# Two-layer mixture kernel: skip sums from two parts, block products summed in pairs, experts' tail rows and rotated keys in other ways, and three changed orders

## The chip, the cores and the metric

The kernel runs on one core of one Trainium2 chip. The metric is the device time of one execution in microseconds (us). All data is fp32.

## The reference

Input x is 16 batches of 256 positions and 512 channels. Four layers follow each other, each on a layer norm of the sum so far.

```python
# 1. gated long convolution: for each of 32 groups of 8 rows
kv = v[:, :, :, None, :] * x2[:, :, None, :, :]            # 8 x 8 products
y  = irfft(rfft(kv) * rfft(k))[..., :L] + kv * skip        # causal convolution, and a skip term
out = einsum('bhijl,bhil->bhjl', y, x1)                    # weighed sum over i
# 2. mixture of 8 experts (the best 2 by gates) and a shared expert
# 3. attention with compressed keys and a rotated part, 16 heads, 9 positions of look-back
k_rope = rope(kv_c @ W_kr)
# 4. dense feed-forward: 512 -> 2048 -> 512, gelu
```

## The kernel before

Each engine has one written-out stream of instructions, with waits on counters. Matmuls that must be exact to fp32 are either one fp32 matmul or three fp32r matmuls: an operand is split into a high part (a copy rounded to fp32r) and a low part (the difference), and high x high, low x high and high x low are summed.

**Convolution.** `NHC` = 32 steps h. A step has two halves u and four output blocks lb of 128 positions, so eight blocks y; each block has its own bank of four `m.Y`. ScalarE norms the rows (`norm`), TensorE turns them (`turn_v`), GpSimd forms the products kf (`product`, L1246), ScalarE their high part kh (`split`), and VectorE or GpSimd the low part kl (`low`, L961 and L1251). TensorE convolves (`conv`, L508 to L516). VectorE's `gather_i` multiplies a block by the context (L971) and reduces over i (L977); TensorE's `turn_out` and VectorE's `finish` make the rows. The skip term is apart: VectorE's `weigh` makes w = xn * skip * ctx (L949), TensorE multiplies w by a fixed 0/1 matrix in fp32 (`skip_sums`, L495), and `skips` multiplies by the context. GpSimd adds the input (`residual`, L1233). Statistics of step h+2 are VectorE's (`stats`, L928 to L932), their power GpSimd's (`power`, L1217). The finished rows of earlier steps are normed (`stats_rows`, `shift_rows`, `norm_rows`), turned (`turn_rows`, L534), and give gate logits, from which `best` and, every eight steps, `choose` pick two experts and their gates.

In a step, VectorE's order is written by hand:

```python
if u == 1 and lb == 2 and h + 2 < NHC: stats(h + 2)
if u == 0 and lb == 0 and more: weigh(h + 1)
if u == 1 and lb == 3 and h + 2 < NHC: shift(h + 2)
gather_i(h, u, lb, UNITS[n] if n < len(UNITS) and lb == 0 else None)   # L971, low, L977
```

**Experts.** After the shared expert (`hidden`, `second`, with `ranks`, `by_head` and `biases` set between its 64 blocks), 71 tiles of 128 rows go through their expert (`tile_first`, `turn_hidden`, `tile_second`, L710). The tile's second bias is gathered into one of four buffers (`tile_bias`, L1346), which the store of four tiles ago must have left, and `tile_out` adds to it (L1194).

**Attention.** 16 batches of 16 heads; TensorE's stream runs scores, turns and sums of successive heads, with the projections of later heads or batches between. Three banks pass from user to user in the order of `misc_order`. In batch 0 the weights of each head are made as well, from factors that SyncE loads into a ring (`factors`, L1461; `weights`, L1682 to L1685). SyncE also stores the mixed rows (`keep`, L1466). `krope` (L1576) makes the keys' rotated part.

**Dense.** 8 groups of 16 blocks; the next group's rows are normed and turned (`dense_stats`, `dense_norm`, `dense_turn`, L2316) beside blocks 3 to 11 of the present one.

Of the kernel before, what the change touches and what calls it, by code (L numbers as in the profile page):

```python
# [96 lines left out]
def front_memory(nc, ctx, m):  # L97
# [48 lines left out]
    m.z = c("z", [128, 3, 512])  # L146
# [31 lines left out]
    c("pad", [128, 3688])  # L178
# [12 lines left out]
    keep("gap", [128, 544])  # L191
    w1 = keep("w1", [128, 2, NE, 1024], F32R)
# [14 lines left out]
def attention_memory(nc, ctx, m):  # L207
# [4 lines left out]
    t("gap", [128, 512])  # L212
# [52 lines left out]
    m.pr = t("pr", [128, 2, 2, 256])  # L265
    m.smf = m.sm[:, :, :].rearrange("p a b -> p (a b)")
# [76 lines left out]
def sync_front(sp, w, K):  # L343
# [93 lines left out]
    for n in range(STEPS + 2):  # L437
# [40 lines left out]
def tensor_front(pe, w, K):  # L478
# [75 lines left out]
    skip_sums(0)  # L554
    for h in range(NHC):
        more = h < LAST
        for u in range(2):
            for lb in range(4):
# [83 lines left out]
    for n in range(STEPS + 2):  # L642
# [14 lines left out]
        if n == 9:  # L657
            by_head()
        if n == 11:
# [73 lines left out]
def scalar_front(ac, w, K):  # L733
# [17 lines left out]

    def turned_v(h):
# [52 lines left out]
    for n in range(4):  # L805
        split(*UNITS[n])
    for h in range(NHC):
        more = h < LAST
        for u in range(2):
            for lb in range(4):  # L810
# [15 lines left out]
                if u == 1 and lb == 0 and h > 8 and h % 8 == 1:  # L826
                    choose(h // 8 - 1)
                if h == LAST and u == 1 and lb in (1, 2):
                    shared_rows(lb - 1)
                if h and u == 1 and lb == 2:  # L830
                    norm_rows(h - 1)
                if h == LAST and u == 1 and lb == 3:
# [23 lines left out]
    for n in range(STEPS + 2):  # L856
# [10 lines left out]
        if n == 9:  # L867
# [3 lines left out]
        if n == 11:  # L871
# [47 lines left out]
def vector_front(ve, w, K):  # L919
# [23 lines left out]
    def weigh(h):  # L943
# [4 lines left out]
        w.wait_ge(*PE["psk", h - 2])  # L948
# [14 lines left out]
    def gather_i(h, u, lb, between):  # L963
# [44 lines left out]
    def choose(c):  # L1008
# [13 lines left out]
        ve.tensor_tensor(cv, m.oh[:, 0, r, :], m.oh[:, 1, r, :], ALU.add).then_inc(*VE("cnt", c))  # L1022
        w.wait_ge(*AC["exp", c])
# [17 lines left out]
    filter_lo()  # L1041
    w.wait_ge(*GP["onef"])
# [7 lines left out]
    skips(0)  # L1050
    for h in range(NHC):
        more = h < LAST
        for u in range(2):
            for lb in range(4):
# [14 lines left out]
                if u == 1 and lb == 0 and h > 8 and h % 8 == 1:  # L1069
                    choose(h // 8 - 1)  # L1070
                if h == LAST and u == 1 and lb == 0:
# [74 lines left out]
    for n in range(STEPS + 2):  # L1146
# [63 lines left out]
def gpsimd_front(gp, w, K):  # L1210
# [71 lines left out]
    for n in range(4):  # L1282
# [3 lines left out]
        if n == 2:  # L1286
            residual(0)
# [53 lines left out]
    def tile_bias(j):  # L1341
        w.wait_ge(*Q[f"y{j % 4}"]["ys", j - 4])
# [28 lines left out]
def misc_order():  # L1371

    out = [("keys", 0), ("values", 0), ("krope", 0)]
# [4 lines left out]
    for h in range(4):  # L1378
        weights(h)
    out.extend([("turn", 0, 0), ("turn", 0, 1)])  # L1380
# [73 lines left out]
def sync_attention(sp, w, K):  # L1454
# [54 lines left out]
    keep(1)  # L1509
    for N in range(TOTAL + 4):  # L1510
# [22 lines left out]
def tensor_attention(pe, w, K):  # L1533
# [154 lines left out]
    values(0)  # L1688
    krope(0)
    for h in range(4):  # L1690
# [56 lines left out]
def scalar_attention(ac, w, K):  # L1747
# [78 lines left out]
    w.wait_ge(*K.PE["m2", TILES - 1])  # L1826
    keys(0)
# [54 lines left out]
def vector_attention(ve, w, K):  # L1882
# [159 lines left out]
    w.wait_ge(*K.PE["m2", TILES - 1])  # L2042
    keys(0)
# [91 lines left out]

def gpsimd_attention(gp, w, K):
# [51 lines left out]
    rope_weights()  # L2188
# [160 lines left out]
def sync_dense(sp, w, K):  # L2349
# [285 lines left out]
```

## Time and profile before

| | |
|---|---|
| timed runs | 3155.25, 3163.14, 3162.99 us, median 3162.99 |
| profiled execution | 3159.11 us, span 3157.4 us |
| TensorE busy | 3094.9 us (98%) |
| VectorE busy | 2206.7 us (70%) |
| ScalarE busy | 1216.9 us (39%) |
| GpSimd busy | 1157.0 us (37%) |
| granted TensorE clock, mean | 0.995 of full speed |
| DMA | 87 GB/s over the span |

The shares are averages over four unlike stages. Between 56 and 580 us, in the convolution, TensorE is busy 519.3 us of 524, VectorE 480.5, GpSimd 461.9 and ScalarE 170.4. A row's "idle before" names what ended the engine's wait. Successive instructions of an engine overlap a little, so the place that one takes is the distance from its start to the next one's start.

### The profile page before, as it was taken

What the parts mean: (1) busy time and instruction counts of PE and PEld (TensorE: products, weight loads), DVE (VectorE), ACT (ScalarE), POOL (GpSimd) and SP (SyncE); (2) the same over time, 40 slices, a digit from 0 to 9 for tenths busy, and PEclk for the clock granted to TensorE, in tenths of its full rate; (3) what the DMA queues carried; (4) which work ended last, traced back from release to release, by engine and by line L of the source; (5) the groups of instructions that cost most, each with busy time, mean ns of one, the idle gap of its engine ahead of it and who ended that gap; (6) DMA issues with size and microseconds to landing.
All of it is one profiled execution on the core that took longest, in us unless ns stands there. A gap on an engine that the chain in (4) does not pass through costs nothing.

```text
span 3157.4 us, 49339 instructions
## 1 busy us (share of the span) xinstructions
PE 3094.9 (98%) x18197; PEld 2652.9 (84%) x18197; DVE 2206.7 (70%) x5732; ACT 1216.9 (39%) x2882; POOL 1157.0 (37%) x1176
## 2 busy tenths in 40 slices
PE   8999999999999789999999999999999999999999
PEld 5667676789899579999999999999998788888887
DVE  7999999756555678888888888888888433333332
ACT  3333333333444345555555555555555311111111
POOL 8988888455344422222222222222201011100110
PEclk9999999999999999999999999999999999999999
DMA  4444432288677621111111111111101200000000
GB/s 144 141 126 142 124 118 87 74 281 306 213 229 227 228 74 55 48 48 41 47 48 48 48 48 42 40 48 42 40 28 57 87 27 27 27 27 27 28 14 14
DMA packets 124973, 277.67 MB, mean 88 GB/s; under 512 B 18312, under 2 KB 18960, under 8 KB 124736
## 3 DMA queue, kind: packets, MB, share of 16 engines
q1 hardware_dynamic: 95712, 178.54, 17.7%
q0 software_dynamic: 29024, 95.97, 9.1%
q8 instruction: 148, 2.42, 0.3%
q14 instruction: 89, 0.73, 0.1%
HBM read 170.04 MB, written 104.42 MB: 87 GB/s over the span
## 4 chain that ended last, share of the span: by engine, by line
PE 91%; DVE 4%; DMA 2%; POOL 1%; ACT 1%; issue 1%; SPq 0%; POOLq 0%; DVEq 0%
PE f_Y L508 5%; PE t_U L1673 4%; PE t_U L1674 4%; PE g_O L2404 4%; PE g_O L2403 4%; PE g_O L2402 4%; PE g_PH L2388 4%; PE g_PH L2390 4%; PE t_U L1675 4%; PE g_PH L2389 4%; PE t_T L1649 3%; PE f_Y L514 3%; PE f_Y L516 3%; PE f_Y L513 3%; PE t_PO L1659 2%; PE t_PO L1660 2%
## 5 line engine op out<-in xcount | busy, mean ns | idle before, releaser
L1798 ACT ACTIVATE t_pr<-t_sm,t_nb 128x256 f32<-128x256 f32 x512 | 256.6, 502 | 407.8 <-DVE t_nb L2003 407.8
L2169 POOL TENSOR_TENSOR t_r<-t_r 128x256 f32<-128x256 f32 x128 | 94.7, 740 | 741.4 <-DVE t_r L1982 419.9
L2460 DVE CAST g_hh<-g_hf 128x512 fp32r<-128x512 f32 x128 | 62.2, 486 | 408.2 <-PE g_O L2404 404.4
L1246 POOL TENSOR_TENSOR c_kf<-c_vt,c_ct 128x512 f32<-128x512 f32 x256 | 297.5, 1179 | 4.4 <-PE f_Y L508 4.4
L2431 ACT ACTIVATE g_hf<-g_PH,b1g 128x512 f32<-128x512 f32 x128 | 88.2, 689 | 501.1 <-PE g_PH L2390 501.1
L2013 DVE TENSOR_SCALAR t_pr<-t_pr,t_rw 128x256 f32<-128x256 f32 x512 | 239.8, 468 | 18.1
L513 PE MATMUL f_Y<-c_kh,c_th 128*128 128x512 f32 x448 | 224.1, 500 | 4.8 <-ACT c_kh L737 2.8
L2388 PE MATMUL g_PH<-g_xh,g_w 128*128 128x512 f32 x512 | 202.6, 396 | 0.0
L1673 PE MATMUL t_U<-t_voh,t_oth 128*128 128x512 f32 x512 | 202.3, 395 | 0.0
L1674 PE MATMUL t_U<-t_voh,t_otl 128*128 128x512 f32 x512 | 201.6, 394 | 0.0
L1675 PE MATMUL t_U<-t_vol,t_oth 128*128 128x512 f32 x512 | 200.5, 392 | 0.0
L2390 PE MATMUL g_PH<-g_xl,g_w 128*128 128x512 f32 x512 | 199.9, 390 | 0.0
L2389 PE MATMUL g_PH<-g_xh,g_w 128*128 128x512 f32 x512 | 199.7, 390 | 0.0
L2404 PE MATMUL g_O<-g_w,g_hh 128*128 128x512 f32 x512 | 199.3, 389 | 0.0
L2402 PE MATMUL g_O<-g_w,g_hh 128*128 128x512 f32 x512 | 199.2, 389 | 0.0
L2403 PE MATMUL g_O<-g_w,g_hl 128*128 128x512 f32 x512 | 199.2, 389 | 0.0
L2003 DVE CUSTOM_DVE_ANT_0 t_sm<-t_S,t_mk 128x256 f32<-128x256 f32 x512 | 194.3, 416 | 4.5 <-PE t_S L1641 3.2
L508 PE MATMUL f_Y<-c_kf,c_t 128*128 128x512 f32 x384 | 185.4, 591 | 0.0
L1751 ACT ACTIVATE t_pth<-t_T 128x512 fp32r<-128x512 f32 x256 | 152.8, 597 | 74.2 <-PE t_T L1649 72.7
L977 DVE TENSOR_REDUCE c_R<-c_z 128x64 f32<-128x512 f32 x256 | 174.9, 683 | 6.7
L2017 DVE TENSOR_TENSOR t_ptl<-t_T,t_pth 128x512 fp32r<-128x512 f32 x256 | 175.3, 685 | 3.9 <-ACT t_pth L1751 1.4
L516 PE MATMUL f_Y<-c_kl,c_th 128*128 128x512 f32 x448 | 178.0, 397 | 0.0
(340 smaller groups left out, 9765.5 us busy)
## 6 DMA issues: line engine op xcount, KB each, us to landing
xs<-c_zero SPq DMA_DIRECT2D x71, 256.0 KB, 4.5
f_xg<-xs SPq DMA_DIRECT2D x71, 256.0 KB, 3.4
ys<-f_yt POOLq DMA_DIRECT2D x71, 256.0 KB, 3.4
f_xg<-xn SPq DMA_DIRECT2D x40, 256.0 KB, 5.3
c_xt<-x SPq DMA_DIRECT2D x32, 256.0 KB, 3.5
c_cr<-ctx SPq DMA_DIRECT2D x32, 256.0 KB, 3.9
c_ct<-ctxh SPq DMA_DIRECT2D x32, 256.0 KB, 4.5
c_t<-kt SPq DMA_DIRECT2D x32, 256.0 KB, 4.8
```

What stands on the lines that cost most here:

```text
L508: t = pe.matmul(Y, m.t[:, h % 3, c], m.kf[:, v, mb, :], start=False, stop=mb == lb)
L513: pe.matmul(Y, m.th[:, s, c], m.kh[:, v, mb, :], start=mb == 0, stop=False)
L1246: gp.tensor_tensor(o, iv, ic, ALU.mult).then_inc(*GP("kv", n))
L1673: pe.matmul(o, m.oth[:, N % 3, tt], m.voh[:, h, :], start=h == 0, stop=False)
L1674: pe.matmul(o, m.otl[:, N % 3, tt], m.voh[:, h, :], start=False, stop=False)
L1675: i = pe.matmul(o, m.oth[:, N % 3, tt], m.vol[:, h, :], start=False, stop=h == NH - 1)
L2388: pe.matmul(o, m.w1[0][k][:, kk, :], m.xh[:, s, kk, :], start=kk == 0, stop=False)
L2389: pe.matmul(o, m.w1[1][k][:, kk, :], m.xh[:, s, kk, :], start=False, stop=False)
L2390: i = pe.matmul(o, m.w1[0][k][:, kk, :], m.xl[:, s, kk, :], start=False, stop=kk == 3)
L2402: pe.matmul(o, m.hh[:, n % 2, c], m.w2[0][k], start=k == 0, stop=False)
L2403: pe.matmul(o, m.hl[:, n % 2, c], m.w2[0][k], start=False, stop=False)
L2404: i = pe.matmul(o, m.hh[:, n % 2, c], m.w2[1][k], start=False, stop=k == BLOCKS - 1)
```

## The change

- `skip_sums`: w is split into wh (ScalarE, `weighed_hi`) and wl (VectorE, `weighed_lo`), and two fp32r matmuls with the 0/1 matrix replace the fp32 one.
- `gather_i`: the product buffers are four, and one reduction sums two blocks' products after every second block.
- `choose` moves two or three blocks later, and its second half is a function of its own, `gates`, one step later still (block 1 of step 10, 18, 26). In the shared stage `by_head`, `biases` and what goes with them move from blocks 9 and 11 to 11 and 13.
- The last four tiles' bias rows are gathered into buffers of their own, after the last tile's first product.
- `krope`: six fp32r matmuls from split weights (`wkh`, `wkl`) and the split keys that exist already, for two in fp32; in batch 0 it follows the weights of head 0.
- Orders: the low part of the rotation weights is made in the tiles' stage (`rope_weights_lo`); batch 0's mix, statistics and norm are interleaved; `keep(1)` follows four factor loads; a group's dense turns are three blocks later; the dense b2 and second rows are loaded behind one more weight fetch.

```diff
 # tensor_front
     def skip_sums(h):
-        w.wait_ge(*GP["ones"])
-        w.wait_ge(*VE["w", h])
+        w.wait_ge(*VE["ones"])
+        w.wait_ge(*AC["wsh", h])
         w.wait_ge(*VE["sx", h - 1])
-        pe.matmul(m.PSK[:, :], m.ones_b, m.w[:, h % 2, :], start=True, stop=True).then_inc(*PE("psk", h))
+        pe.matmul(m.PSK[:, :], m.ones_r, m.wh[:, h % 2, :], start=True, stop=False)
+        w.wait_ge(*VE["wsl", h])
+        pe.matmul(m.PSK[:, :], m.ones_r, m.wl[:, h % 2, :], start=False, stop=True).then_inc(*PE("psk", h))
...
-        if n == 9:
+        if n == 11:
             by_head()
-        if n == 11:
+        if n == 13:
             biases()
 # scalar_front
+    def weighed_hi(h):
+        s = h % 2
+        w.wait_ge(*VE["w", h])
+        w.wait_ge(*PE["psk", h - 2])
+        copy(m.wh[:, s, :], m.w[:, s, :]).then_inc(*AC("wsh", h))
...
+                if u == 0 and lb == 0 and more:
+                    weighed_hi(h + 1)
 # vector_front
+    def weighed_lo(h):
+        s = h % 2
+        w.wait_ge(*AC["wsh", h])
+        ve.tensor_tensor(m.wl[:, s, :], m.w[:, s, :], f32(m.wh[:, s, :]), ALU.subtract).then_inc(*VE("wsl", h))
...
-        zz = m.z[:, y % 3, :].rearrange("p (b j i) -> p b j i", i=8, j=8)
+        zz = m.z[:, y % 4, :].rearrange("p (b j i) -> p b j i", i=8, j=8)
         w.wait_ge(*PE["y", y])
-        w.wait_ge(*VE["red", y - 3])
+        w.wait_ge(*VE["red", (y - 4) | 1])
         ve.tensor_tensor(zz, iv, ic, ALU.mult).then_inc(*VE("z", y))
         if between:
             low(*between)
+        if lb % 2 == 0:
+            return
...
-        rr = m.R[:, s, lb, 64 * u:64 * u + 64].rearrange("p (b j) -> p b j", j=8)
-        ve.tensor_reduce(rr, zz, AXX, ALU.add).then_inc(*VE("red", y))
+        z2 = m.z[:, y % 4 - 1:y % 4 + 1, :].rearrange("p q (c i) -> p q c i", i=8)
+        ve.tensor_reduce(m.R[:, s, lb - 1:lb + 1, 64 * u:64 * u + 64], z2, AXX, ALU.add).then_inc(*VE("red", y))
...
+                if u == 0 and lb == 2 and more:
+                    weighed_lo(h + 1)
...
-                if u == 1 and lb == 0 and h > 8 and h % 8 == 1:
+                if u == 1 and lb == 3 and h > 8 and h % 8 == 1:
                     choose(h // 8 - 1)
+                if u == 0 and lb == 1 and h > 8 and h % 8 == 2:
+                    gates(h // 8 - 1)
 # gpsimd_front
     for n in range(4):
         product(*UNITS[n])
         if n == 1:
             low(*UNITS[n])
-        if n == 2:
-            residual(0)
...
     def tile_bias(j):
-        w.wait_ge(*Q[f"y{j % 4}"]["ys", j - 4])
+        if j < TILES - 4:
+            w.wait_ge(*Q[f"y{j % 4}"]["ys", j - 4])
+        else:
+            w.wait_ge(*PE["m1", TILES - 1])
...
     for n in range(TILES + LAG):
-        if LAG - 2 <= n < TILES + LAG - 2:
+        if LAG - 2 <= n < TILES - 1:
             tile_bias(n - LAG + 2)
+        if n == TILES - 1:
+            for j in range(TILES - 4, TILES):
+                tile_bias(j)
         if n >= LAG:
             tile_store(n - LAG)
+        if n == TILES:
+            rope_weights_lo(gp, w, K)
 # sync_attention
     load(1)
-    keep(1)
     for N in range(TOTAL + 4):
...
         if N + EARLY + 2 < NH:
             factors(N + EARLY + 2)
+        if N == 3:
+            keep(1)
 # tensor_attention
     def krope(b):
-        w.wait_ge(*A["kc", b])
+        w.wait_ge(*A["wkh"])
+        w.wait_ge(*V["wkl"])
+        w.wait_ge(*A["kh", b])
+        w.wait_ge(*V["kl", b])
         M = take("krope", b)
         for z in range(2):
-            i = pe.matmul(M[:, 256 * z:256 * z + 256], m.wkr[:, z, :], m.kc[:, :], start=True, stop=True)
+            o = M[:, 256 * z:256 * z + 256]
+            pe.matmul(o, m.wkh[:, z, :], m.kch[:, s, :], start=True, stop=False)
+            pe.matmul(o, m.wkl[:, z, :], m.kch[:, s, :], start=False, stop=False)
+            i = pe.matmul(o, m.wkh[:, z, :], m.kcl[:, s, :], start=False, stop=True)
 # vector_attention
     mix(0, 0)
+    stats(0, 0)
     mix(0, 1)
-    stats(0, 0)
+    norm(0, 0)
     stats(0, 1)
-    norm(0, 0)
     norm(0, 1)
 # tensor_dense
-            if g + 1 < GROUPS and k in (5, 7, 9, 11):
-                dense_turn(pe, w, K, 4 * (g + 1) + (k - 5) // 2)
+            if g + 1 < GROUPS and k in (8, 10, 12, 14):
+                dense_turn(pe, w, K, 4 * (g + 1) + (k - 8) // 2)
```

## Rows read from the trace of the kernel before

**Rows 1.** Waits of TensorE, whole span: us in total, times, longest.

```profile
PE t_M L1554 <- DVE t_r L1914: 9.0, 1, 9.0
PE t_M L1682 <- DMA t_xo<-fac: 8.2, 1, 8.2
...
PE f_PV L534 <- ACT c_xb L789: 6.1, 4, 1.6
PE f_Y L710 <- DVE f_yt L1194: 5.4, 4, 1.7
PE f_PV L623 <- DVE f_idc L1122: 2.9, 1, 2.9
...
PE g_PM L2316 <- DVE g_xn L2295: 2.4, 1, 2.4
```

**Rows 2.** The chain in order of time, convolution: start us, us, what.

```profile
65.62 0.23 PE f_Y L513
...
409.73 0.86 PE f_PSK L495 x2
...
463.62 0.86 PE f_PSK L495 x2
```

**Rows 3.** Timeline of VectorE, one step: start us, us, instruction, idle before.

```profile
403.02 0.88 DVE L961 TENSOR_TENSOR c_kl<-c_kf,c_kh 128x512 fp32r<-128x512 f32 x1 [1.02 <-ACT c_kh L737]
403.82 0.68 DVE L977 TENSOR_REDUCE c_R<-c_z 128x64 f32<-128x512 f32 x1
404.42 0.68 DVE L971 TENSOR_TENSOR c_z<-f_Y,c_ct 128x512 f32<-128x512 f32 x1
405.13 0.69 DVE L977 TENSOR_REDUCE c_R<-c_z 128x64 f32<-128x512 f32 x1
...
407.22 0.69 DVE L971 TENSOR_TENSOR c_z<-f_Y,c_ct 128x512 f32<-128x512 f32 x1
...
410.08 1.15 DVE L961 TENSOR_TENSOR c_kl<-c_kf,c_kh 128x512 fp32r<-128x512 f32 x1
411.16 0.67 DVE L977 TENSOR_REDUCE c_R<-c_z 128x64 f32<-128x512 f32 x1
...
415.73 0.15 DVE L932 TENSOR_SCALAR c_rs<-c_ag 128x1 f32<-128x1 f32 x1
...
420.98 0.88 DVE L961 TENSOR_TENSOR c_kl<-c_kf,c_kh 128x512 fp32r<-128x512 f32 x1 [1.03 <-ACT c_kh L737]
```

**Rows 4.** Timeline of GpSimd, the same step.

```profile
406.03 1.06 POOL L1246 TENSOR_TENSOR c_kf<-c_vt,c_ct 128x512 f32<-128x512 f32 x1
407.36 2.10 POOL L1246 TENSOR_TENSOR c_kf<-c_vt,c_ct 128x512 f32<-128x512 f32 x2 [0.26 <-PE f_Y L508]
409.41 1.28 POOL L1227 TENSOR_TENSOR c_tl<-c_t,c_th 128x512 fp32r<-128x512 f32 x1
410.65 1.73 POOL L1251 TENSOR_TENSOR c_kl<-c_kf,c_kh 128x512 fp32r<-128x512 f32 x1
...
415.96 0.55 POOL L1217 TENSOR_TENSOR c_rs<-c_rs,mhalf 128x1 f32<-128x1 f32 x1 [1.45 <-DVE c_rs L932]
```

**Rows 5.** Timeline of VectorE, an operation of 256 elements.

```profile
1062.65 0.41 DVE L1941 TENSOR_TENSOR t_kvl<-t_M,t_kvh 128x256 fp32r<-128x256 f32 x1
```

**Rows 6.** Timelines of VectorE and GpSimd: low parts beside GpSimd.

```profile
28.19 4.24 DVE L961 TENSOR_TENSOR c_kl<-c_kf,c_kh 128x512 fp32r<-128x512 f32 x1
...
118.99 1.28 POOL L1227 TENSOR_TENSOR c_tl<-c_t,c_th 128x512 fp32r<-128x512 f32 x1
...
119.02 1.79 DVE L961 TENSOR_TENSOR c_kl<-c_kf,c_kh 128x512 fp32r<-128x512 f32 x1
```

**Rows 7.** Timeline of VectorE, end of a choose.

```profile
193.82 1.27 DVE L1028 TENSOR_TENSOR f_gac<-c_sm,f_gac 128x8 f32<-128x8 f32 x1
```

**Rows 8.** Timeline of GpSimd, the attention's first gather.

```profile
1065.76 1.00 POOL L2149 DMA_INDIRECT t_xT<-ys,idx  x1 [2.52 <-DMA ys<-f_yt]
```

**Rows 9.** Waits of SyncE, 1030 to 1130 us.

```profile
SPq L81 <- POOL t_xt L2160: 24.2, 1, 24.2
```

More of the change, by code:

```diff
@@ L177, in front_memory @@
     m.ob = c("ob", [8, 2, 512])
-    c("pad", [128, 3688])
+    m.wh = c("wh", [128, 2, 512], F32R)
+    m.wl = c("wl", [128, 2, 512], F32R)
+    m.ones_r = c("ones_r", [128, 128], F32R)[:, :]
+    c("pad", [128, 1000])
     sw = c("sw", [128, 8192], F32R)
@@ L191, in front_memory @@
     keep("gap", [128, 544])
+    with ExitStack() as late:
+        sb(nc, late, "f_gap3", [128, 13168])
+        m.yx = sb(nc, late, "f_yx", [128, 4, 512])
     w1 = keep("w1", [128, 2, NE, 1024], F32R)
@@ L210, in t @@
         return sb(nc, ctx, f"t_{name}", shape, dt)
-    t("gap", [128, 512])
+    t("gap", [128, 256])
+    m.wkl = t("wkl", [128, 2, 128], F32R)
     with ExitStack() as low:
@@ L337, in turn_at, with out_rows, bias_landed @@
     return None
+def out_rows(m, j):
+    return m.yt[:, j % 4, :] if j < TILES - 4 else m.yx[:, j % 4, :]
+def bias_landed(j):
+    return f"v{j % 4}" if j < TILES - 4 else f"vx{j % 4}"
 def sync_front(sp, w, K):
@@ L553, in tensor_front @@
     turn_v(0)
-    skip_sums(0)
     for h in range(NHC):
@@ L565, in tensor_front @@
                     skip_sums(h + 1)
+                if u == 0 and lb == 2 and h == 0:
+                    skip_sums(0)
                 if u == 0 and lb == 0 and h > 1:
@@ L804, in scalar_front @@
     turned_v(0)
-    for n in range(4):
-        split(*UNITS[n])
+    split(*UNITS[0])
+    split(*UNITS[1])
+    weighed_hi(0)
     for h in range(NHC):
@@ L831, in scalar_front @@
                     norm_rows(h - 1)
+                if u == 1 and lb == 3 and h > 8 and h % 8 == 1:
+                    choose(h // 8 - 1)
                 if h == LAST and u == 1 and lb == 3:
@@ L1022, in choose, with gates @@
         ve.tensor_tensor(cv, m.oh[:, 0, r, :], m.oh[:, 1, r, :], ALU.add).then_inc(*VE("cnt", c))
+    def gates(c):
+        r = slice(8 * c, 8 * c + 8)
+        S_ = m.sm[:, c % 2, :, :]
         w.wait_ge(*AC["exp", c])
@@ L1049, in vector_front @@
     low(0, 0, 0)
-    skips(0)
+    weighed_lo(0)
     for h in range(NHC):
@@ L1064, in vector_front @@
                     finish(h - 1)
+                if u == 0 and lb == 2 and more:
+                    weighed_lo(h + 1)
+                if u == 0 and lb == 3 and h == 0:
+                    skips(0)
                 if u == 1 and lb == 1 and more:
@@ L1068, in vector_front @@
                     best(h - 2)
-                if u == 1 and lb == 0 and h > 8 and h % 8 == 1:
+                if u == 1 and lb == 3 and h > 8 and h % 8 == 1:
                     choose(h // 8 - 1)
+                if u == 0 and lb == 1 and h > 8 and h % 8 == 2:
+                    gates(h // 8 - 1)
                 if h == LAST and u == 1 and lb == 0:
@@ L1159, in vector_front @@
             choose(3)
+        if n == 6:
+            gates(3)
         if n == 8:
@@ L1308, in gpsimd_front @@
                     filter_lo(h + 1)
+                if u == 1 and lb == 0 and h == 0:
+                    residual(0)
                 if u == 1 and lb == 2 and more:
@@ L1371, in misc_order @@
 def misc_order():
-    out = [("keys", 0), ("values", 0), ("krope", 0)]
+    out = [("keys", 0), ("values", 0)]
     def weights(h):
@@ L1379, in misc_order @@
         weights(h)
+        if h == 0:
+            out.append(("krope", 0))
     out.extend([("turn", 0, 0), ("turn", 0, 1)])
@@ L1688, in tensor_attention @@
     values(0)
+    weights(0)
     krope(0)
-    for h in range(4):
+    for h in range(1, 4):
         weights(h)
@@ L2130, in vector_attention, with rope_weights_lo @@
             dense_turned_lo(ve, w, K, 3)
+def rope_weights_lo(gp, w, K):
+    m = K.t
+    w.wait_ge(*K.A["wrah"])
+    gp.tensor_tensor(m.wrl[:, :], m.wqr[:, 0, :], f32(m.wra[:, :]), ALU.subtract).then_inc(*K.G("wra"))
 def gpsimd_attention(gp, w, K):
@@ L2368, in sync_dense @@
             dense_fetch(sp, w, K, k + 6)
+        if n == 0:
+            w.wait_ge(*P["vo", TOTAL - 1, 1])
+            w.wait_ge(*V["add", 2 * B - 1])
+            w.wait_ge(*Q["to"]["out", B - 1])
+            sp.dma_start(m.b2s[:, :], K.d["f1b2"]).then_inc(*Q["gb1"]("b2"))
+            load(1)
         if n >= 2 and (n - 2) % BLOCKS == BLOCKS - 1 and (n - 2) // BLOCKS + 2 < GROUPS:
@@ L2426, in scalar_dense @@
             dense_weights_hi(ac, w, K, k + 3)
-        if g + 1 < GROUPS and k in (5, 7, 9, 11):
-            dense_turned_hi(ac, w, K, 4 * (g + 1) + (k - 5) // 2)
+        if g + 1 < GROUPS and k in (8, 10, 12, 14):
+            dense_turned_hi(ac, w, K, 4 * (g + 1) + (k - 8) // 2)
         w.wait_ge(*P["dph", n])
@@ L2468, in gpsimd_dense @@
         g, k = divmod(n, BLOCKS)
-        if n < DSTEPS and g + 1 < GROUPS and k in (3, 5, 7, 9):
-            dense_power(gp, w, K, 4 * (g + 1) + (k - 3) // 2)
+        if n < DSTEPS and g + 1 < GROUPS and k in (6, 8, 10, 12):
+            dense_power(gp, w, K, 4 * (g + 1) + (k - 6) // 2)
         if n < 2:
@@ L2535 @@
               "cc", "n0", "n1", "w0", "w1", "ti", *(f"g{i}" for i in range(RING)), "q0", "q1", "a0", "a1", *(f"s{i}" for i in range(RING)),
-              *(f"l{i}" for i in range(4)), *(f"y{i}" for i in range(4)), *(f"v{i}" for i in range(4)),
+              *(f"l{i}" for i in range(4)), *(f"y{i}" for i in range(4)), *(f"v{i}" for i in range(4)), *(f"vx{i}" for i in range(4)),
               "tx", "tct", "tsg", "to", "txo", *(f"tyg{i}" for i in range(4)), "tx2", "tc", "tc2", "tw0", "tw1", *(f"tm{i}" for i in range(4)),
```

50 lines of the change are left out of this document (24 added, 26 removed).

## Prediction

> **What bounds the kernel now.** The page came first: TensorE is busy almost all the span (the table above), so a change pays only if it takes time from TensorE's own stream or from its waits. The table of waits for TensorE puts 34 us of its idle time on six lines [rows 1]; the rest is small. Then I read the convolution (to about 590 us) as a chain in order of time. One channel step h takes (463.62 - 409.73)/3 = 17.96 us. TensorE is hardly ever idle in it but for three waits of 1.6 at L534. The skip product, one fp32 matmul of 512 columns, holds it 0.86, an fp32r one 0.23 [rows 2].
>
> Who comes second in that stage decides this change. VectorE's timeline over one step [rows 3] and GpSimd's [rows 4] show a closed loop. VectorE ends the variance for step h+2 at 415.73 + 0.15 = 415.88. GpSimd sat 1.45 us waiting for it, then makes in order the power, a product, a residual sum and the product that ScalarE splits; 5.10 after the variance VectorE starts that product's low part c_kl (420.98), having waited 1.02. Call K the start of this c_kl (403.02), T the start of the fourth block's product (407.22). K to T is 4.20; the places of its instructions make 4.02 (c_kl 0.80, three reductions of 0.60, two products of 0.71), so 0.18 is waiting for TensorE. T to the variance's end is 8.66; then 5.10. The loop alone turns in 17.78, only 0.18 quicker than TensorE. The change has to be judged by both.
>
> **Convolution, TensorE.** Fp32 skip product to two fp32r: 0.86 - 2 x 0.234 = 0.39 less per step, 17.57 if nothing else binds.
>
> **Convolution, VectorE.** A reduction of 512 takes a place of 0.60 (403.82 to 404.42), a product and the wait of the reduction behind it 0.71 (404.42 to 405.13) [rows 3]. 256 elements more cost 0.27 (0.68 against 0.41, [rows 5]), so a paired reduction takes 0.60 + 2 x 0.27 = 1.14; its bounds are 0.87 (nothing for the fixed part twice over) and 1.20 (two of now). `weighed_lo` has the form of c_kl: two operands in SBUF, 0.80 at the least disturbed.
>
> But such a subtraction waits for GpSimd. C_kl at 410.08 took 1.15: GpSimd was in a subtraction until 410.65, and VectorE's next instruction came 0.51 after that [rows 3, 4]. At 119.02 it came 0.03 after GpSimd's subtraction had begun and took 1.79; at 28.19 it took 4.24 [rows 6]. The Trainium skill, "SBUF — State Buffer", section "Who interferes with whom", says that a VectorE instruction with two SBUF inputs and a GpSimd one that reads SBUF exclude each other, the second waiting in full. By that rule, the trace agrees: 1.15 and 1.79; without it the sum below would be 17.4 and TensorE's 17.57 the bound, with it 19.33.
>
> The new order from K, with GpSimd's product at K + 3.01 to 4.07 (406.03) [rows 4]:
> - c_kl 0.80, product and paired reduction 0.71 + 1.14, product 0.60: `weighed_lo` is reached at K + 3.25, inside GpSimd's product. It gets its turn at 4.07; T comes 0.51 later, K + 4.58.
> - From T to the next c_kl were 2.86; the reduction in between grows by 0.54: 3.40, so K + 7.98. GpSimd goes on 0.41 to 0.45 after VectorE took its turn (its subtraction at 410.65 took 1.73 instead of 1.28): two products 2.05 and a subtraction 1.24 end at 7.77 to 7.82, and the next subtraction holds until 9.06. C_kl misses the gap by 0.15 to 0.2, waits until 9.06, and what follows starts at 9.57.
> - From there to the variance's end were 415.88 - 411.16 = 4.72; a reduction goes (-0.60), another grows (+0.54): 4.66, so 14.23. Then 5.10 as before: weigh comes at 2.6 after the variance, as now, and `weighed_hi` on ScalarE is over before the split. K' = K + 19.33.
>
> VectorE's loop would set the period at 19.33, 1.37 longer than now. TensorE would wait 19.33 - 17.57 = 1.76 per step, at L534, the one line of the loop at which it already waits. In steps 1 to 8 GpSimd has one more subtraction in that place; the same sum gives 19.3. The loop exists where step h+2 has statistics: 29 turns, +39.7. The last two steps gain 0.39 each, TensorE ends about 1.2 ahead of VectorE, the head gains perhaps 1 by the moved residual sum (bounds +4 and -4, the wait of 4.24 is there): -3.0.
>
> **Choose and gates.** Choose's chain on VectorE delays the rows' shift and makes three of the four waits at L534, 4.7 of 6.1 [rows 1]. They go. But three times 1.6 (gates; its last product alone is 1.27 [rows 7]) now stand in the loop, and some 0.7 (an estimate: five small instructions) where choose pushes weigh back: 6.9 - 4.7 = +2.2.
>
> Convolution: 39.7 - 3.0 + 2.2 = +38.9.
>
> **`by_head`, `biases`.** TensorE waits 2.9 for the places [rows 1]; two blocks later they are long there: -2.9. What is late next is nothing in the trace before the tiles.
>
> **Experts' tail, first turn.** The last four tiles' bias rows no longer wait for a store four tiles back; they are four gathers in a row on GpSimd, about 1.3 each, behind the last first product. Of the 5.4 at L710 the first two waits stay, the last two (2.3) go. The stores queue behind these gathers and the moved 2.35 us subtraction of rotation weights, and still end about 4 earlier, so the attention's first gather (1065.76, waiting for the last landing [rows 8]) does too. VectorE is free some 3 earlier, mixes without that subtraction beside it, and norms after one statistic instead of two. The wait of 9.0 at L1554 shrinks and starts earlier: -5.6 for both, bounds -2.3 (only L710) and -11.3.
>
> **Store of the mixed rows.** The 8.2 at L1682 is for a factor load stuck on SyncE behind `keep(1)`, which waits 24.2 for GpSimd's mix [rows 1, 9]. Four factor loads pass it now. Late next is VectorE, a step or so of 1 us behind, and the stored rows before batch 1's first norm: -7.5, bounds -4 and -9.
>
> **Rotated keys.** Two fp32 products of 256 columns (as many as one of 512, 0.86) become six fp32r of 256 (half of 0.234): 0.70. 16 batches: -2.6 (bounds 0 and -3.5). The new waits, c_kch and its low part, are two heads old by then.
>
> **Dense.** The 2.4 at L2316 goes, the turns being three blocks later; five half-steps remain before their use: -2.4. The fetch set ahead of b2 lies under a busy TensorE: 0.
>
> Outside the convolution: -2.9 - 5.6 - 7.5 - 2.6 - 2.4 = -21.0. With +38.9: +17.9. The profiled execution took 3159.1 (span 3157.4 and 1.7 around it), inside the three timed runs, whose median is 3163.0: 3159.1 + 17.9 = 3177.0.
>
> **Rivals.**
> - The next c_kl catches the gap. 0.15 to 0.2 us decide, near the error of my places; a paired reduction under 0.95 would do. Loop 4.58 + 3.40 + 0.51 + 4.66 + 5.10 = 18.25, +0.29 x 29 = 8.4; total 3159.1 + 8.4 - 0.8 - 21.0 = 3145.7. For it: most c_kl show 0.88. Against: the sum.
> - VectorE does not wait in these two places; TensorE's 17.57 binds. 29 x -0.39, choose's 4.7 and 1 of the head: -17; 3121, faster. It decides if lock waits are below 0.15 per step in sum.
> - The waits are of the 4.24 kind: one more operation of GpSimd (1.24) in a third of the steps, +12: 3189.
> - The gains after the convolution are half, because a transfer or VectorE follows up: 3187.
>
> Chances: forecast 0.53, gap caught 0.18, no waits 0.14, long waits 0.08, half gains 0.07. The forecast's own range is 3168 to 3186. Over all, without the second rival and the far end of the third: 3138 to 3192. Within 0.3% (9.5 us) is what a measurement of this kernel can't tell from no change. Faster: 0.14 and 0.11 of the 0.18, 0.25; same: the rest of it and a little of the forecast's low end, 0.10; slower 0.65.
>
> **What would show it.** Skip products at 0.23 each; 19.3 from one step's skip product to the next against 17.96; a wait at L534's turn in nearly every step, for ScalarE's c_xb; `weighed_lo` at 1.4, the c_kl of the first unit at 1.6 to 1.8; no waits at the places of L623, L1682 (8.2) and L2316; L1554 at 4 to 6. I am wrong if c_kl and the new subtraction show 0.88: then the period is below 18.2.

## The result, and the profile after

The changed kernel takes 3192.7 us (median of four runs, 3190.5 to 3195.3); the kernel before, beside it, 3162.6. The ratio is 1.0103, with a 95% interval of 1.0090 to 1.0116: slower by 30 us, where +17.9 was forecast. Its profiled execution took 3195.3 (span 3192.5), 36.2 more than that of before: the one is the longest of its four, the other lies 3.4 under its median, so 6 of these 36 are the choice of executions.

The waits of TensorE in the changed kernel, whole span (us in total, times, longest):

```profile
PE f_PV L553 <- ACT c_xb L815: 44.6, 30, 1.8
PE t_M L1615 <- DVE t_r L1985: 7.3, 2, 6.2
PE f_PT L505 <- ACT c_xn L770: 7.3, 1, 7.3
PE f_PSK L512 <- DVE c_sk L990: 5.6, 1, 5.6
```

L553 is L534 of before [rows 1]: four waits (6.1 in all) have become thirty (44.6). The waits of L623, of L1682 (8.2) and of L2316 are gone, and L1554, now L1615, still stands for 7.3. L505's 7.3 is nothing new: it is at the program's start, and before had 7.5 there (L488), which [rows 1] leave out. L512's 5.6 is new.

One step on VectorE, changed kernel, from one K to the next:

```profile
433.86 0.88 DVE L995 TENSOR_TENSOR c_kl<-c_kf,c_kh 128x512 fp32r<-128x512 f32 x1 [1.02 <-ACT c_kh L757]
...
435.37 1.22 DVE L1013 TENSOR_REDUCE c_R<-c_z 128x128 f32<-128x1024 f32 x1
...
437.10 1.37 DVE L984 TENSOR_TENSOR c_wl<-c_w,c_wh 128x512 fp32r<-128x512 f32 x1
438.39 0.68 DVE L1005 TENSOR_TENSOR c_z<-f_Y,c_ct 128x512 f32<-128x512 f32 x1
...
441.78 1.68 DVE L995 TENSOR_TENSOR c_kl<-c_kf,c_kh 128x512 fp32r<-128x512 f32 x1
443.38 0.68 DVE L1024 BATCH_NORM_STATS2 c_st<-c_xt 128x6 f32<-128x512 f32 x1
...
447.89 0.15 DVE L961 TENSOR_SCALAR c_rs<-c_ag 128x1 f32<-128x1 f32 x1
...
453.13 0.88 DVE L995 TENSOR_TENSOR c_kl<-c_kf,c_kh 128x512 fp32r<-128x512 f32 x1 [1.02 <-ACT c_kh L757]
```

And GpSimd in the same step:

```profile
440.38 1.29 POOL L1277 TENSOR_TENSOR c_tl<-c_t,c_th 128x512 fp32r<-128x512 f32 x1
441.63 1.28 POOL L1301 TENSOR_TENSOR c_kl<-c_kf,c_kh 128x512 fp32r<-128x512 f32 x1
```

Set beside [rows 3, 4]: `weighed_lo` (L984) is reached at K + 3.24 (forecast 3.25), T at K + 4.53 (4.58), the next c_kl at K + 7.92 (7.98). The gap between GpSimd's two subtractions was at 441.63; c_kl came 0.15 later and took 1.68, until the second one was over. The variance ends at K + 14.18 (14.23), K returns after 19.27 (19.33). The skip products, 0.23 each as forecast:

```profile
439.74 0.39 PE L512 MATMUL f_PSK<-c_wh,c_ones_r 128*128 128x512 f32 x1
439.97 0.39 PE L514 MATMUL f_PSK<-c_wl,c_ones_r 128*128 128x512 f32 x1
459.04 0.39 PE L512 MATMUL f_PSK<-c_wh,c_ones_r 128*128 128x512 f32 x1
```

The places are 0.23 apart, the duration 0.39 overlaps the next. The table says in which stage time was lost or won: how much later than in before the same instruction of TensorE starts, from the timelines of the profiled executions (us; the experiments' columns are read below).

```
                                  after    e1    e4    e5    e6    e7   e10
end of convolution (last L553)    +45.3  +5.5  -0.8  -1.0  +0.3  +0.2  -0.4
last shared product               +41.1  +0.8  -5.5  -4.6  -4.1  -4.3  -5.1
tiles: last first product         +41.6  +3.3  -5.3  -1.5  -2.4  -1.5  -2.0
first latent keys                 +40.1  +1.7  -4.0  -1.1  -3.2  -1.7  -1.5
turn(0,0)                         +40.4  +2.0  -3.7  -0.7  -5.6  -1.4  -2.0
first scores                      +42.8  +2.9  -2.6  +0.2  -3.6  -0.4  -0.8
keys of batch 2                   +41.6  -3.0  -6.1   0.0  -7.6  -5.6  -6.7
last scores                       +39.3  -5.2  -8.4  -2.2  -9.8  -7.8  -9.0
end                               +35.1  -9.4 -12.6  -6.4 -14.0 -12.0 -13.2
```

### The profile page after: what moved, and what is told of

Its sections match the earlier page's. It is cut to its first block, busy times and chain, and to the rows that moved or that the text cites. A ratio compares the mean times of both kernels' runs of the same rounds, so it can differ in the third digit from the quotient of the medians.

```text
span 3192.5 us, 49352 instructions
## 1 busy us (share of the span) xinstructions
PE 3088.6 (97%) x18229; PEld 2652.3 (83%) x18229; DVE 2249.0 (70%) x5638; ACT 1235.2 (39%) x2915; POOL 1157.6 (36%) x1176
## 4 chain that ended last, share of the span: by engine, by line
PE 75%; DVE 17%; POOL 4%; DMA 2%; ACT 1%; issue 1%; SPq 0%; POOLq 0%; DVEq 0%
DVE c_R L1013 4%; PE g_PH L2463 4%; PE g_PH L2465 4%; PE g_PH L2464 4%; PE g_O L2479 4%; PE g_O L2478 4%; PE g_O L2477 4%; PE t_U L1741 4%; PE t_U L1742 4%; PE t_U L1743 4%; PE t_T L1717 3%; DVE c_z L1005 3%; POOL c_kf L1296 2%; DVE c_kl L995 2%; PE t_S L1706 2%; PE t_PO L1727 2%
## 5 line engine op out<-in xcount | busy, mean ns | idle before, releaser
L2535 DVE CAST g_hh<-g_hf 128x512 fp32r<-128x512 f32 x128 | 54.7, 427 | 430.3 <-PE g_O L2479 426.6
L1296 POOL TENSOR_TENSOR c_kf<-c_vt,c_ct 128x512 f32<-128x512 f32 x256 | 306.2, 1217 | 0.0
L2084 DVE TENSOR_SCALAR t_pr<-t_pr,t_rw 128x256 f32<-128x256 f32 x512 | 241.9, 473 | 18.1
L532 PE MATMUL f_Y<-c_kh,c_th 128*128 128x512 f32 x448 | 212.0, 473 | 4.5 <-ACT c_kh L757 4.5
L533 PE MATMUL f_Y<-c_kh,c_tl 128*128 128x512 f32 x448 | 178.4, 398 | 0.0
```

The lines of the kernel that those rows point to most:

```text
L1296: gp.tensor_tensor(o, iv, ic, ALU.mult).then_inc(*GP("kv", n))
L2084: ve.tensor_scalar(m.pr[:, N % 2, t, :], m.pr[:, N % 2, t, :], m.rw[:, k4, 1:2], None, ALU.mult).then_inc(*V("nm", x))
```

## The experiments

There are fourteen, labelled e1 to e15 (there is no e8); the tenth kernel of some expectations is e10. Each ratio is against the kernel before run beside it; that one's medians lay between 3158.9 and 3159.9.

**e1, the skip product in fp32 again.** `weighed_hi` and `weighed_lo` go with it; the paired reductions stay.

```diff
     def skip_sums(h):
-        w.wait_ge(*AC["wsh", h])
+        w.wait_ge(*VE["w", h])
-        pe.matmul(m.PSK[:, :], m.ones_r, m.wh[:, h % 2, :], start=True, stop=False)
-        pe.matmul(m.PSK[:, :], m.ones_r, m.wl[:, h % 2, :], start=False, stop=True)
+        pe.matmul(m.PSK[:, :], m.ones_b, m.w[:, h % 2, :], start=True, stop=True)
```

> The changed kernel with the skip product as before (one fp32 product of 0.86 on TensorE, no weighed_hi, no weighed_lo), all else as changed, paired reductions too. The theory (weighed_lo waits for a GpSimd product and pushes the next c_kl past its gap): without it the fourth block's product comes at K + 3.25 and VectorE's loop needs 0.80 + 2.45 + 3.40 + 0.9 + 4.66 + 5.10 = 17.3, so TensorE's 17.96 binds again: period 17.9 to 18.0, some 37 us less than the changed kernel, 3152 to 3160. Rival (the paired reductions alone lengthen VectorE's part, since the one that holds c_kl back is now 1.2 long): period stays above 18.8, 3178 or more.

Measured: 3148.5, ratio 0.9966 (0.9953 to 0.9978), 44 less than the changed kernel and 3.5 under the range. Skip products come 17.97 apart from step 10 on, as the theory said, but for the steps with a choose; in steps 4 to 9 every second one is 18.4 to 18.5. The fp32r product, meant to save 0.39 a step, costs 1.31 through its low part.

**e2, one reduction for each block, the skip product split.**

```diff
-        if lb % 2 == 0:
-            return
-        z2 = m.z[:, y % 4 - 1:y % 4 + 1, :].rearrange("p q (c i) -> p q c i", i=8)
-        ve.tensor_reduce(m.R[:, s, lb - 1:lb + 1, 64 * u:64 * u + 64], z2, AXX, ALU.add)
+        rr = m.R[:, s, lb, 64 * u:64 * u + 64].rearrange("p (b j) -> p b j", j=8)
+        ve.tensor_reduce(rr, zz, AXX, ALU.add)
```

> The changed kernel with one reduction for each block instead of the pairs; the skip product stays split. The theory (a gap between two GpSimd subtractions is missed by 0.2 us): T comes at K + 4.58 as in the changed kernel, but c_kl of the next step is reached at T + 2.86 = K + 7.44, takes the gap at 7.8, and the period is 18.1 to 18.3, 28 us less than the changed kernel, 3160 to 3168. Rival (no gap, VectorE is simply short of time): the four single reductions cost as much as the two paired ones, period 19.2 to 19.4, 3190 to 3197.

Measured: 3178.0, ratio 1.0055 (1.0039 to 1.0072), between the two ranges. Steps 2 to 9 take 18.11 (one 17.67), as the sum has it; from step 10 on 18.2 and 19.35 come mixed. VectorE of e2, two of those later steps, and the GpSimd product that starts in each as `weighed_lo` is reached:

```profile
248.13 0.88 DVE L995 TENSOR_TENSOR c_kl<-c_kf,c_kh 128x512 fp32r<-128x512 f32 x1 [1.02 <-ACT c_kh L757]
252.16 0.68 DVE L984 TENSOR_TENSOR c_wl<-c_w,c_wh 128x512 fp32r<-128x512 f32 x1
255.62 0.99 DVE L995 TENSOR_TENSOR c_kl<-c_kf,c_kh 128x512 fp32r<-128x512 f32 x1
...
266.35 0.88 DVE L995 TENSOR_TENSOR c_kl<-c_kf,c_kh 128x512 fp32r<-128x512 f32 x1 [1.02 <-ACT c_kh L757]
270.37 1.62 DVE L984 TENSOR_TENSOR c_wl<-c_w,c_wh 128x512 fp32r<-128x512 f32 x1
274.76 1.20 DVE L995 TENSOR_TENSOR c_kl<-c_kf,c_kh 128x512 fp32r<-128x512 f32 x1
...
285.69 0.88 DVE L995 TENSOR_TENSOR c_kl<-c_kf,c_kh 128x512 fp32r<-128x512 f32 x1 [1.02 <-ACT c_kh L757]
```

```profile
252.16 1.61 POOL L1294 TENSOR_TENSOR c_kf<-c_vt,c_ct 128x512 f32<-128x512 f32 x1
...
270.37 1.07 POOL L1294 TENSOR_TENSOR c_kf<-c_vt,c_ct 128x512 f32<-128x512 f32 x1
```

`weighed_lo` is reached at K + 4.03 and 4.02, both times within 0.01 of the start of a GpSimd product. Once it slips in and takes 0.68, and it is the product that gets longer (1.61; K to K 18.22); once it waits and takes 1.62 (K to K 19.34). What the trace can't tell apart decides over 1.1: neither theory's one period, but a knife's edge, and the mechanism is who gets the turn, not VectorE's load, which is the same in both steps.

**e3 and e9, the low part in the shadow.** `weighed_lo(h + 1)` is moved from behind the third block to just ahead of the c_kl at K, where VectorE waits 1.02 for ScalarE; e9 has single reductions and choose in its old place as well.

```diff
+        if u == 0 and lb == 0 and h < LAST:
+            weighed_lo(h + 1)
         if between:
             low(*between)
```

> The changed kernel with weighed_lo moved from behind the third block to where VectorE waits 1.02 us for ScalarE, just ahead of the c_kl at K. The theory (the loop runs over VectorE from K to the variance; what stands between the variance and K is in the shadow of GpSimd and ScalarE): K comes at most 0.5 later, T at K + 3.25, period 17.6 to 17.9, 3140 to 3155. Rival (any two-operand subtraction of VectorE costs its wait wherever it stands, and GpSimd is held up by it): period 18.8 or more, over 3178.

> The changed kernel with weighed_lo in the shadow, one reduction per block, and choose where it was (no gates). Theory: VectorE's loop before, where TensorE did not hold it, turned in 17.65; the low part in the shadow adds nothing to 0.1, so the period is TensorE's 17.57 to 17.75, 0.2 to 0.4 less than before in 29 steps, and the time 3136 to 3144. Rival (K comes late enough that c_kl meets GpSimd's product, as in the pairs' version): 18.0 to 18.1, 3150 or so.

Measured: e3 3157.9, ratio 0.9991 (0.9982 to 1.0001), period 18.04; e9 3157.5, ratio 0.9987 (0.9977 to 0.9996), period 18.11. So the place of one instruction is worth 35 us here, with the same load on VectorE, but both are above the 17.9 and 17.75 that I expected, and e3 3 over its range in time: K comes in its old place after the variance (5.08), but the low part ahead of it had held up GpSimd's three products (4.46 in all, 4.03 in the changed kernel), so c_kl meets one and takes 1.33. For e9 the rival's period was right, its time 7 too low.

**e12, a low part with one operand.** `weighed_lo` is a plain copy of c_w; the kernel leaves the subtraction out, so its skip sums are not those of the reference.

```diff
-        ve.tensor_tensor(m.wl[:, s, :], m.w[:, s, :], f32(m.wh[:, s, :]), ALU.subtract)
+        ve.tensor_copy(m.wl[:, s, :], m.w[:, s, :])
```

> The changed kernel with weighed_lo replaced by a plain copy of c_w into the same tile (one operand in SBUF instead of two; the low part is then not what the reference needs). Theory (only an instruction with two SBUF operands waits for GpSimd's): the copy takes 0.6 at most and never waits, T at K + 3.7 to 3.9, c_kl of the next step reached at K + 7.2, in or just ahead of the gap at 7.3 to 7.8, period 17.6 to 18.2. Rival (VectorE's share of the step is too large, lock or no lock): 18.8 to 19.3.

Measured: 3182.8 (one run), period 19.0. VectorE and GpSimd of e12:

```profile
426.95 0.88 DVE L995 TENSOR_TENSOR c_kl<-c_kf,c_kh 128x512 fp32r<-128x512 f32 x1 [1.02 <-ACT c_kh L757]
...
430.20 1.11 DVE L984 CAST c_wl<-c_w 128x512 fp32r<-128x512 f32 x1
...
434.61 1.68 DVE L995 TENSOR_TENSOR c_kl<-c_kf,c_kh 128x512 fp32r<-128x512 f32 x1
```

```profile
433.22 1.29 POOL L1277 TENSOR_TENSOR c_tl<-c_t,c_th 128x512 fp32r<-128x512 f32 x1
434.47 1.27 POOL L1301 TENSOR_TENSOR c_kl<-c_kf,c_kh 128x512 fp32r<-128x512 f32 x1
```

My theory fell in its first half: a copy with one SBUF operand waits too (1.11; where nothing was in its way it took 0.42). The second half held: c_kl missed the gap at 434.47 by 0.14 and paid 1.68. The period is the rival's (18.8 to 19.3), but not for its reason: without the copy's wait of 0.7, c_kl would by this sum have come 0.6 ahead of the gap. The Trainium skill, "SBUF — State Buffer", section "SBUF: two separate sides", counts VectorE's faster two-port modes among what excludes GpSimd beside instructions with two SBUF inputs, and an fp32 copy within SBUF among those modes; the trace agrees, and I had left that half of the rule out.

**e13 and e14, the low part on GpSimd.** Single reductions, everything behind the convolution as in e10 (below); `weighed_lo` is a subtraction of GpSimd behind the third block's product (the lines below, in GpSimd's program). In e14 this holds from step 10 on, with the fp32 product ahead of that.

```diff
+                if u == 0 and lb == 2 and more:
+                    weighed_lo(h + 1)
```

> The best of the rest (tenth kernel) with the skip product from two parts, single reductions, and weighed_lo made by GpSimd behind the third block's product, where it is 1.45 ahead of the variance it waits for. Theory: a GpSimd subtraction is 1.27, so it fits in those 1.45; VectorE has no new instruction; period TensorE's 17.57 to 17.75, 6 to 11 quicker than the tenth: 3132 to 3137. Rival: GpSimd's later products push ScalarE's split and c_kl into another subtraction; period 18.1 to 18.6, 3147 to 3160.

> The tenth kernel (3145.9) with the skip product in two parts only from step 10 on, its low part on GpSimd. The thirteenth run showed why: in steps 1 to 8, where GpSimd also makes a low part of the shared weights (shared_lo), the loop took 18.90, later 17.66. Theory: 22 steps at 17.58 to 17.67 instead of 17.97, -0.3 each: 6 less, 3139 to 3141. Rival: VectorE's own loop of 17.65 was already what set the rest of the step, and the gain stays under 2: 3144 to 3147.

Measured: e13 3158.1, ratio 1.0004 (0.9992 to 1.0016): 18.90 in steps 3 to 10, 17.57 to 17.67 later, so the time is the rival's and the later period the theory's. e14 3146.4, ratio 0.9956 (0.9943 to 0.9970): 17.66 from step 10 on. Yet its convolution ends only 2.3 earlier than e10's: in each step with a choose the skip products are 20.4 to 22.1 apart, where they were 19.8, where TensorE waits 2.6 to 2.8 for c_xb instead of 1.6. Of 5.7 gained between the chooses 3.8 go at them. The period was the theory's, the time the rival's. Behind the choose of 22.1 three steps take 17.57 to 17.59, TensorE's own sum, and the fourth 17.66 again: that fits a loop of VectorE of 17.66 as the second bound, 0.3 under the 17.97 of before.

**e15, the pairs alone** (on e10).

> The tenth kernel with the blocks summed in pairs and nothing else of the convolution's part. Theory (the pairs are harmless alone: VectorE's loop of 17.3 to 17.7 stays under TensorE's 17.97): skip products 17.97 apart, 3144 to 3147. Rival (the first experiment's early steps, every second one 18.4 to 18.5, are the pairs' own doing): four or five steps 0.5 longer, 3148 to 3150.

Measured: 3148.6, ratio 0.9965 (0.9952 to 0.9978). 17.97 from step 10 on, but 18.27 to 18.45 in steps 5, 7 and 9, and its convolution ends 1.9 later than e10's. The rival was right: the early steps were the pairs' own doing, the rest is harmless.

**e11, only choose and gates moved** (on e4).

```diff
-                if u == 1 and lb == 0 and h > 8 and h % 8 == 1:
+                if u == 1 and lb == 3 and h > 8 and h % 8 == 1:
                     choose(h // 8 - 1)
+                if u == 0 and lb == 1 and h > 8 and h % 8 == 2:
+                    gates(h // 8 - 1)
```

> The kernel without the convolution's part (3146.0) with only choose moved to the last block and gates to a later step. Forecast: +2.2 if VectorE's loop were the bound; here TensorE is, VectorE has some 0.3 per step to catch up, and choose's stalls of 4.7 should go: 3142 to 3146, skip products 17.97 apart but in two steps of each three longer by under 1. By the first experiment (steps with choose and gates cost 9.4 over the others, before 5.4): 3149 to 3150.

Measured: 3151.4, ratio 0.9978 (0.9967 to 0.9988). Two steps of 18.82 and 20.32 where one of 19.76 was: +3.2 against +1.8, three times, +4.2. That is more than either expectation had: the move costs, although TensorE is the bound here. VectorE's groups in the changed kernel (count, busy us, mean ns), 190 to 640 us:

```profile
L1054 DVE TENSOR_TENSOR c_oh<-c_iota,c_sm 128x64 f32<-128x64 f32 x3 | 3.5, 1155 | 0.0
L1051 DVE TENSOR_TENSOR c_sm<-c_mx 128x8 f32<-128x8 f32 x3 | 3.0, 990 | 0.1
```

The same two took 219 and 174 ns in before. In before GpSimd stood idle beside them (2.28 us, until 193.78); in the new place it makes three products in a row (213.57 to 216.70), and an instruction of 8 or 64 elements waits for each (the other of 64 elements took 1101 ns on average).

**e4, e5, e6, e7, e10, the part behind the convolution.** e4 has the convolution of before and all else of the change. e5 puts `keep(1)` back ahead of the loads; e6 puts the first rotated keys back ahead of the first weights; e7 puts the bias ring and the rotation weights' subtraction back; e10 is e6 and e7 together.

```diff
+    keep(1)
     for N in range(TOTAL + 4):
...
-        if N == 3:
-            keep(1)
```

```diff
-    weights(0)
     krope(0)
-    for h in range(1, 4):
+    for h in range(4):
         weights(h)
```

> The convolution as before (skip product, reductions, choose, residual of the first step), everything that the change does behind it kept. By my forecast this part is worth -21.0: 3138. By the trace of the changed kernel, where the shift against before falls from 45.3 at the end of the convolution to 35.1 at the end, it is worth -10: 3149 to 3153.

> The kernel without the convolution's part, with the store of batch 1's mixed rows back ahead of the factor loads. The forecast priced the move at -7.5: the time would be 3153. The trace of the kernel without the convolution's part shows the wait of 8.2 gone but 4.7 of it given back within 30 us (VectorE waits for this same store to land before batch 1's norm): by it the move is worth 3 to 4, 3149 to 3150.

> As above without the convolution's part, the store late, and on TensorE the first rotated keys ahead of the first head's weights as before (still from parts). Theory: the wait of 2.9 for t_mb comes from the new order, because VectorE has the keys' rotation ahead of the first head's low parts; back in the old order the wait is under 1 and the first turn 2 us earlier; 3143 to 3144 if nothing gives it back. Rival: the turn is set by the gathered rows and VectorE's mix, then the wait only moves and the time stays at 3146.

> As above without the convolution's part, with the four last tiles' bias rows in the ring of four again and the rotation weights' subtraction back behind the first gathers. Forecast: 5.6 slower, 3151 to 3152. By the trace (the shift went from -5.3 at the start of the tail to -3.9 at its end, so the four gathers in a row cost 1.4; the mix without the subtraction beside it starts later but runs 2 quicker): within 2 us of the kernel it undoes, 3144 to 3148.

> Convolution as before, tail as before (ring of four, rotation weights' subtraction behind the first gathers), rotated keys from parts but ahead of the first weights; moved stay the store of batch 1, by_head and biases, the dense turns. Theory: the tail's edits cost 1.5 and the new order of the first weights 2.7 in the traces, so this is 3 to 4 quicker than the kernel without the convolution's part (3146.0): 3142 to 3143. Rival: such gains are given back before the second batch, as part of the store's was: 3145 to 3147.

Measured: e4 3146.0, ratio 0.9955 (0.9939 to 0.9972); e5 3153.0, 0.9979 (0.9969 to 0.9989); e6 3146.3, 0.9958 (0.9941 to 0.9975); e7 3150.4, 0.9969 (0.9956 to 0.9981); e10 3145.9, 0.9961 (0.9947 to 0.9976). The part is worth 14, not 21, nor the 10 of the changed kernel's trace; e5 came out where the forecast had it, e6 and e10 where their rivals had them, e7 between its two; and e4, e6, e10 and e14 beat both kernels by the same within their intervals.

The table warns of reading more out of these medians. From the last shared product to the last first product of the tiles all these kernels run the same code, and in the profiled executions the shift grows there by 0.2 (e4) to 3.1 (e5, e10), in e2 by 4.0. Of the 7.0 between e4 and e5, 3.8 stand there already. So e6 and e7 against e4 are inconclusive as times.

## Why the prediction was wrong

The direction and the mechanism of the large term were right, and the time was 0.7 above the range. Between the spans 17.2 are missing (+17.9 against +35.1), between the medians 12.2 (+30.1). The forecast came true together with what it had only as a rival, that the gains behind the convolution are half.

The steps that failed, by size in the spans: the store of the mixed rows (forecast -7.5, measured +1.2 over its stretch), the head and the end of the convolution (-3.0, +5.0), the first turn (-5.6, -1.3), choose and gates (+2.2, +3.5). The period (39.7, 36.7), `by_head` (-2.9, -4.2) and the dense turns (-2.4, -4.2) came out better than forecast.

**Convolution, +45.3 against +38.9.** The period was right: 28 steady turns at 19.28 against 17.97 are +36.7 (forecast 1.37 x 29 = 39.7). The missed gap sets it, as three sides show: without the low part 17.97 (e1), with the gap sometimes caught 18.1 to 18.2 (e2), with the low part elsewhere 18.04 (e3). The step that failed is "the last two steps gain 0.39 each, TensorE ends about 1.2 ahead of VectorE, the head gains perhaps 1: -3.0". Measured is +2.9 by the fourth skip product and +2.1 behind the last. The head, VectorE and then GpSimd:

```profile
24.25 4.65 DVE L984 TENSOR_TENSOR c_wl<-c_w,c_wh 128x512 fp32r<-128x512 f32 x1
30.67 0.68 DVE L990 TENSOR_TENSOR c_sk<-c_cr,f_PSK 128x512 f32<-128x512 f32 x1
```

```profile
24.01 3.11 POOL L1296 TENSOR_TENSOR c_kf<-c_vt,c_ct 128x512 f32<-128x512 f32 x3
27.09 1.25 POOL L1277 TENSOR_TENSOR c_tl<-c_t,c_th 128x512 fp32r<-128x512 f32 x1
```

The 4.24 of [rows 6] was not gone but had found the new instruction: it waited for four operations of GpSimd in a row, of which only the first was running when it came, and had its turn at their end. `skips(0)` stands behind it, and TensorE's second skip product waits 5.6 for that. Without the low part (e1) the fourth skip product comes 0.7 earlier than in before, so the +2.9 comes with the split product. Of the +2.1 at the end the paired reductions make 0.8 (e1 and e15 have it too); the rest stays open. I had named a bound of +4 for the head and taken -1.

**Choose and gates, +3.5 against +2.2.** Steps with a choose cost 3 x 2.97 = 8.9 over the others (skip products), before 3 x 1.80 = 5.4. Mis-sized: "five small instructions, 0.7" were three of 1.0 to 1.15. The lock that I priced for `weighed_lo` holds for them too.

**Behind the convolution, -10.2 against -21.0.**

- `by_head`: -4.2 to the last shared product (forecast -2.9), then +0.6 in the tiles before the last first product. The wait was priced, and not what follows it. TensorE in before, at the wait and behind it (the third number from the right is its granted clock):

```profile
632.00:635.00 3.00, 0.08 (x2) 0.06 (x2) 2.79 (x8) 0.00 (x0) 1.06 (x2) 1.00 0.44 119
635.00:638.00 3.00, 3.00 (x19) 3.00 (x20) 1.02 (x3) 1.78 (x3) 0.00 (x0) 0.65 0.28 74
```

- Experts' tail and first turn: -1.3 (forecast -5.6), and the second turn waits another 1.1. The changed kernel, TensorE and then VectorE:

```profile
1106.90 0.77 PE L1750 MATMUL t_M<-t_fac 128*128 128x128 f32 x2 [2.75 <-DVE t_mb L2109]
1119.09 1.11 PE L1615 MATMUL t_M<-ident,t_r 128*128 128x128 f32 x4 [6.23 <-DVE t_r L1985]
```

```profile
1104.18 0.42 DVE L2021 TENSOR_TENSOR t_krf<-t_M,t_ck 128x256 f32<-128x256 f32 x1 [1.29 <-PE t_M L1644]
...
1106.46 0.29 DVE L2109 TENSOR_TENSOR t_mb<-t_M,t_mb 64x128 fp32r<-64x128 f32 x1
...
1114.14 1.60 DVE L1967 SCALAR_TENSOR_TENSOR t_xt<-t_xT,gat,t_xt 128x512 f32<-128x512 f32 x2
```

The first gather came 1.4 earlier against the latent keys (1104.45, [rows 8]) where I had taken 4, but VectorE reached the mix 43.1 later than in before, where the latent keys are 40.1 later. TensorE now does the first weights ahead of the rotated keys; VectorE still has the keys' rotation first, so t_mb waits for keys that came later, and TensorE for t_mb. I looked at GpSimd's queue and the stores and not at whether VectorE's order followed TensorE's. In e6 the old order brings the turn 1.9 earlier than in e4, in e10 only 0.6 earlier than in e7: so this wait is one cause, and how much of the missing 4.3 it is stays open.
- Store of the mixed rows: the wait of 8.2 is gone, but from turn(0,0) to the third batch's keys the changed kernel loses 1.2 (forecast -7.5). e5, with the store early, loses 0.7; e4 gains 2.4, e1 4.9, e7 4.2. Of the thirteen builds with the late store beside this one, eleven gain 1.5 to 5.0 over before there, and e3 and e11 lose as much as this one. Against e5, the one build with the early store, the move is worth 2 to 6 in the eleven and nothing in these three. VectorE meets the late store before batch 1's norm, as foreseen, and it is late already, its small instructions taking up to 1.2 beside GpSimd's additions:

```profile
1152.94 1.20 DVE L2084 TENSOR_SCALAR t_pr<-t_pr,t_rw 128x256 f32<-128x256 f32 x1
...
1174.18 0.55 DVE L1985 TENSOR_SCALAR t_xt<-t_xt,t_ag,t_rs 128x512 f32<-128x512 f32 x1 [1.77 <-DMA x<-t_xt]
```

L2084 also shows 0.35 two instructions earlier (1152.48). In the changed kernel TensorE waits 2.8 for t_mb at L1676 where it waited 1.1, and its granted clock fell to 0.66 from 1140 to 1145. The same dip, 20 to 25 us after the first turn, stands in e3 and e11 (0.68, 0.66) and in none of the other builds (1.00). The code is not what decides: from the tiles on e1, e2 and e12 have that of this build, e4 that of e11. What does stays open.
- Rotated keys: -2.3 from the third batch's keys to the last scores, in every kernel (forecast -2.6).
- Dense: -4.2, the same in the changed kernel and in all those of the table (forecast -2.4), all of it where before had the wait at L2316. The rows of before say why. Timeline of TensorE, and its granted clock (third from the right) in three stretches:

```profile
2462.06 1.12 PE L2316 MATMUL g_PM<-ident,g_xn 128*128 128x128 f32 x4 [2.41 <-DVE g_xn L2295]
...
2464.25 0.63 PE L2388 MATMUL g_PH<-g_xh,g_w 128*128 128x512 f32 x1
...
2465.95 0.39 PE L2390 MATMUL g_PH<-g_xl,g_w 128*128 128x512 f32 x1
```

```profile
2458.00:2459.50 1.50, 1.50 (x8) 1.02 (x6) 1.39 (x5) 0.00 (x1) 0.68 (x1) 1.00 0.84 309
2459.50:2462.00 2.50, 0.14 (x1) 0.00 (x0) 1.84 (x4) 1.83 (x3) 0.00 (x0) 1.00 0.08 29
2462.00:2465.20 3.20, 3.14 (x10) 2.66 (x11) 1.72 (x4) 1.20 (x3) 0.00 (x0) 0.50 0.49 157
```

After 2.4 idle TensorE ran at 0.50 of its clock, 1.2 GHz, for 3.2 us. I counted the wait and forgot what follows it, here and at `by_head`. Behind the 8.2 at L1682 before had the 0.50 too, for 4.8 us (1119.2 to 1124.0), so even more was to be had there than I took.

## What to carry to other kernels

Before a product is taken off the busiest engine, close the loop of the others: here VectorE's stood 0.3 us a step behind TensorE, so not all of the 0.39 could be had, and the low part on VectorE made it a loss of 1.3. An instruction that shares SBUF with GpSimd is priced by the gap it reaches, to a tenth of a microsecond, and this holds for small ones as for large. When one engine's order changes, put the others' beside it; and a wait that goes can take the slow clock behind it along.

## What the runs showed of the hardware

- A VectorE instruction was held up by four GpSimd operations in a row, three of which began after it had come (4.65 at 24.25). Copies with one operand (1.11), scalar multiplications (1.20) and subtractions of 8 elements (0.99) wait like subtractions of 512, while the products with an operand in PSUM and the paired reductions kept their 0.68 and 1.22.
- A wait of 2.4 of TensorE cost 4.2, with the granted clock at 0.50 behind it; one of 2.9 (at `by_head`) cost 4.7 in e4, with 0.65 behind it.
- From the last shared product to the last first product of the tiles, where the code is the same, the shift against before grew by 0.2 (e4) to 4.0 us (e2), in one profiled execution of each. Whether that goes with the build or with the execution isn't shown. So a difference of under 4 us between two kernels' times can't be laid to an edit by the times alone; it takes the stage that the edit touches.
